# Relation layers with one group in three gathered, two filled from the node table, and the adjacency loop run by three groups

## The reference

```
src, dst = edge_index                         # 103125 edges, dst sorted
h = relu(layernorm(x))                        # 3125 x 128
for W, b, a, g, beta in three layers:         # node layers, 256 wide, and a fourth without the norm
    c = segment_sum((h @ W)[src] * norm, dst) + b
    h = elu(layernorm(c * sigmoid(a)) * g + beta)
x = x + fourth_layer(h)
y = relu(layernorm(x))
for l in range(3):                            # relation layers
    seg = dst * 16 + edge_type
    agg = segment_sum(y[src], seg) / max(count, 1)      # 3125 x 16 x 128
    y = einsum('nrd,rdo->no', agg, W[l]) + y @ root[l] + bias[l]
    y = relu(y) except in the last
out = x + y
```

## Time and profile before

| | us |
|---|---|
| median of 3 runs | 4118.48 (4111.23 to 4122.4) |
| the profiled execution | 4112.04 |
| its span | 4110.3 |
| TensorE busy in the span | 2902.5 (71%) |
| VectorE busy | 2243.8 (55%) |
| ScalarE busy | 1309.5 (32%) |
| GpSimd busy | 1214.9 (30%) |
| relation layers, start to end of the span | 1643 to 4110 |

### The profile page before, as it was taken

The page is one execution under the profiler, slowest core; times in us unless marked ns, Lnnn a source line. Parts: engine busy times, 40 slices in busy tenths (PEclk is TensorE's granted clock), DMA queues, the critical chain, the costliest instruction groups (busy, mean ns, idle before and its releaser), DMA issues.

```text
span 4110.3 us, 80589 instructions
## 1 busy us (share of the span) xinstructions
PE 2902.5 (71%) x25480; PEld 1920.3 (47%) x25481; DVE 2243.8 (55%) x7967; ACT 1309.5 (32%) x3058; POOL 1214.9 (30%) x1251
## 2 busy tenths in 40 slices
PE   3214776777799897677777777777777767777777
PEld 1112333333455554455555555555555545555555
DVE  6667888885634433354445444445444444544444
ACT  0315777775322210222222222222222222222221
POOL 1020000000000000354545543544454444445443
PEclk8557889888899999898999999999999999999999
DMA  0001000001101012533333334333333333333332
GB/s 21 0 23 52 36 36 36 36 36 50 52 20 46 20 51 58 156 112 99 101 115 105 101 91 123 104 109 108 101 102 111 103 105 102 113 101 100 114 100 74
DMA packets 164628, 320.93 MB, mean 78 GB/s; under 512 B 33105, under 2 KB 127676, under 8 KB 154924
## 3 DMA queue, kind: packets, MB, share of 16 engines
q1 hardware_dynamic: 123532, 231.88, 18.2%
q0 software_dynamic: 40992, 87.70, 7.9%
HBM read 274.51 MB, written 44.96 MB: 78 GB/s over the span
## 4 chain that ended last, share of the span: by engine, by line
PE 24%; issue 10%; DMA 10%; DVE 8%; POOL 6%; another core or an unknown queue 1%; DVEq 1%; ACT 0%; SPq 0%; POOLq 0%; ACTq 0%
DMA arena<-pair,arena 9%; PE psum L1922 8%; PE psum L1933 7%; PE psum L1942 6%; POOL arena L1846 6%; DVE arena L2090 3%; DVE arena L2086 3%; DVE arena L2123 1%; DVE arena L2096 1%; PE psum L1903 1%; PE psum L1911 1%; PE psum L1880 1%; DVEq L2123 0%; PE psum L1887 0%
## 5 line engine op out<-in xcount | busy, mean ns | idle before, releaser
L1846 POOL DMA_INDIRECT arena<-pair,arena x1212 | 1162.7, 959 | 1280.9 <-PE psum L1911 655.5
L2034 ACT ACTIVATE arena<-psum 128x512 f16<-128x512 f32 x909 | 477.3, 598 | 1663.4 <-PE psum L1911 1040.3
L1922 PE MATMUL psum<-arena 128*128 128x320 f16 x2424 | 445.1, 334 | 554.5 <-DMA arena<-pair,arena 318.0
L2096 DVE SCALAR_TENSOR_TENSOR arena<-psum,arena,work 128x320 f32<-128x320 f32 x606 | 329.3, 548 | 739.5 <-PE psum L1933 340.0
L1933 PE MATMUL psum<-arena 128*128 128x320 f16 x4242 | 680.7, 316 | 0.0
L1922 PEld LDWEIGHTS psum<-arena 128*128 128x128 f16 x2424 | 232.5, 106 | 733.1 <-issue 589.9
L1933 PEld LDWEIGHTS psum<-arena 128*128 128x128 f16 x4242 | 440.7, 104 | 201.9
L1090 PE MATMUL psum<-arena,h 128*128 128x512 f16 x1750 | 487.2, 384 | 23.5 <-ACT work L1144 15.5
L2090 DVE TENSOR_SCALAR arena<-arena 128x320 f16<-128x320 f16 x2121 | 484.9, 297 | 0.0
L1942 PE MATMUL psum<-arena 128*128 128x160 f32 (+1 forms) x2496 | 359.2, 303 | 50.7 <-issue 36.9
L1091 PE MATMUL psum<-arena,h 128*128 128x128 f16 x1750 | 386.7, 221 | 0.0
(11 more groups left out here) (260 smaller groups left out, 3303.8 us busy)
## 6 DMA issues: line engine op xcount, KB each, us to landing
work<-winv SPq DMA_DIRECT2D x75, 1280.0 KB, 6.2
arena<-pull SPq DMA_DIRECT2D x303, 224.0 KB
pull<-rows SPq DMA_DIRECT2D x101, 224.0 KB
arena<-pair,arena POOLq DMA_INDIRECT x1212
h<-work SPq DMA_DIRECT2D x12, 640.0 KB, 3.3
h<-h POOLq DMA_DIRECT2D x12, 640.0 KB, 7.4
pair<-arena SPq DMA_DIRECT2D x12, 256.0 KB
x_pad<-arena SPq DMA_DIRECT2D x1, 1600.0 KB, 7.3
```

The costliest lines, as they stand in the source:

```text
L1846: e.indirect_dma_start(out=t.msg[:, j, k].rearrange("p h f -> p (h f)"), out_offset=None, in_=d[f"pair_{l}"].rearrange("n h f -> n (h f)") ...
L1922: m = e.matmul(p.psum[:, 0, 0:KEYS], t.msg[:, j, tile, half, :], t.oh[:, j % 2, tile, :], start=(tile == 0 and half == 0), stop=(tile == G ...
L2034: e.activation(t.smsg[:, q, 2 * b:2 * b + 2].rearrange("p k h f -> p (k h f)"), p.psum[:, GATHER + b, :], ACT.Copy).then_inc(s_gv, 1)
L2096: e.scalar_tensor_tensor(t.agg[h][:, :, k % BATCH, :], p.psum[:, k % 2, 0:KEYS].rearrange("p (r w) -> p r w", r=REL), t.back[:, l:l + 1], ...
```

## The change

Three stages are rewritten, and two follow from that.

**Relation layers.** Groups come in threes: one gathered, two filled. 67 threes and one gathered group make a layer, so 68 groups are gathered (101 before) and 134 filled (101 before). The order on TensorE in a three is `sums_gathered`, a fill, `sums_filled`, a fill, `sums_filled`. A turn is 12 groups (4 threes, `TURN`), an apply takes 6 groups (`BATCH`); there are 16 turns and a rest of 10 groups. The first apply of a turn stands in the third three, behind its first fill. POOL gathers two threes ahead: two tiles after `sums_gathered` of three j-2, two after the second fill of three j-2. The sums go to the two banks in turn, and VectorE writes the one-hots in three parts between the means.

**Adjacency loop.** Three groups in an iteration, two of them with slots. ScalarE makes all one-hots of sources. 134 slot matrices are written instead of 101.

**Slots.** All arrays grow from 101 to 134 filled groups.

**Node layers.** ScalarE copies the first half of the products of group i+1 ahead of its work on group i, with a semaphore of its own (`s_z`), and the exponential, the ELU sum and the high half are done in two parts (2 and 3 blocks).

```diff
-PAIRS = EDGE_TILES // GT // 2
+TRIPLES = EDGE_TILES // GT // 3
+FILLED = 2 * TRIPLES
...
-BATCH = 8
-HALF = BATCH // 2
+BATCH = 6
 TURN = 2 * BATCH
-TP = TURN // 2
+TT = TURN // 3
+HALF = TT // 2
+FT = 2 * TT
...
# POOL, relation layers
-        def gathers(l, turn, ready, pairs):
-            held(e, s_pk, ready, passed)
-            for j in pairs:
-                filled = turn * TP + (l * PAIRS + j + 1)
-                summed = turn * TURN + (MM0 + l * NG + 2 * j)
+        def gathers(l, turn, h):
+            held(e, s_pk, turn * 6 + (l * PICKS + 3 * h + 1), passed)
+            for j in range(h * HALF, h * HALF + HALF):
+                summed = turn * TURN + (MM0 + l * NG + 3 * (j - 2) + 1)
+                filled = turn * FT + (GA0 + l * FILLED + 2 * (j - 2) + 3)
                 for k in range(GT):
                     if k == 0:
+                        held(e, s_mm, summed, passed)
+                    if k == 2:
                         held(e, s_ga, filled, passed)
-                    elif k == 2:
-                        held(e, s_mm, summed - 1, passed)
...
# TensorE, relation layers
-            def pairs_of(turn, pairs, ahead):
-                for j in range(pairs):
-                    if j < ahead:
-                        fill(turn, j + 1, PIECES * j)
+            def triples_of(turn, triples, fills):
+                for j in range(triples):
                     sums_gathered(turn, j)
-                    sums_filled(turn, j)
-                    if j % HALF == HALF - 1 or j == pairs - 1:
-                        apply(turn, j // HALF, 2 * (j % HALF + 1))
+                    fill(turn, 2 * j + 1, PIECES * 2 * j)
+                    if j == HALF:
+                        apply(turn, 0, BATCH)
+                    sums_filled(turn, j, 0)
+                    if 2 * j + 2 <= fills:
+                        fill(turn, 2 * j + 2, PIECES * (2 * j + 1))
+                    sums_filled(turn, j, 1)
...
             with e.Fori(0, TURNS) as i:
-                pairs_of(i, TP, TP)
+                triples_of(i, TT, FT)
+                apply(i, 1, BATCH)
...
# VectorE, relation layers
+        def triples_of(l, turn, triples, hots):
+            for j in range(triples):
+                more, gather_more = j + 1 < hots, j + 1 < hots or triples == RT
+                mean(l, turn, 3 * j)
+                if gather_more:
...
+                    hots_gathered((j + 1) % TT)
+                if j == HALF:
+                    adds(l, turn, 0, BATCH)
+                mean(l, turn, 3 * j + 1)
+                if more:
+                    hots_filled((j + 1) % TT, 0)
+                mean(l, turn, 3 * j + 2)
+                if more:
+                    hots_filled((j + 1) % TT, 1)
...
# VectorE, adjacency loop
+        def trio(i, more):
+            e.load(regs, t.gbase[0:1, bass.ds(i * 3, 3)])
+            keys(i * 3 + 2, 2)
+            adds(i * 3, 0)
+            slot_hots(i * 2)
+            keys(i * 3 + 3, 0)
+            adds(i * 3 + 1, 1)
+            slot_hots(i * 2 + 1)
+            ones(i * 2)
+            slot_keys(i * 2, 0)
+            if more:
+                keys(i * 3 + 4, 1)
+            adds(i * 3 + 2, 2)
+            ones(i * 2 + 1)
+            slot_keys(i * 2 + 1, 1)
...
# TensorE, adjacency loop
-        with e.Fori(0, ROUNDS // 2) as i:
-            for par in range(2):
-                r = i * 2 + par
-                turn(r + 1, 1 - par)
-                slot_keys(r, par)
-                place(r + 1, 1 - par)
+        with e.Fori(0, TRIPLES) as i:
+            turn(i * 3 + 1, 1)
+            place(i * 2, 0)
+            turn(i * 3 + 2, 2)
+            slot_keys(i * 2, 0)
+            place(i * 2 + 1, 1)
+            turn(i * 3 + 3, 0)
+            slot_keys(i * 2 + 1, 1)
...
# ScalarE, node layers
+            for k in range(KH):
+                sums(0, k)
             for i in range(GROUPS):
+                early = i + 1 < GROUPS and (KH == 1 or i + 2 < GROUPS)
+                if early:
+                    sums(i + 1, 0)
                 group(i, stays and i == GROUPS - 1)
+                if i + 1 < GROUPS:
+                    for k in range(1 if early else 0, KH):
+                        sums(i + 1, k)
```

More of the change, by code:

```diff
@@ L810, in _, with sources @@
+        trio(TRIPLES - 1, False)
+        e.load(regs[0:1], t.gbase[0:1, ROUNDS - 1:ROUNDS])
+        adds(ROUNDS - 1, 0)
     @block.scalar
     def _(e):
-        e.sem_inc(s_ct, 2 * G)
-        e.sem_inc(s_src, 2)
-        def sources(r, par):
+        e.sem_inc(s_ct, 3)
+        e.sem_inc(s_src, 3)
+        def sources(r, pos):
             held(e, s_st, r + 2, passed)
-            held(e, s_src, r + 2, passed)
-            for k in range(ASCAL):
-                e.activation(t.away[:, k, :], t.iota_h[:, 0:P], ACT.Abs, bias=t.stage[:, par, 0, k:k + 1],
+            held(e, s_src, r + 3, passed)
+            for k in range(GT):
+                e.activation(t.away[:, k, :], t.iota_h[:, 0:P], ACT.Abs, bias=t.stage[:, pos, 0, k:k + 1],
@@ L842, in _, with trio @@
+        def trio(i, more):
+            take(i * 3, 0)
+            sources(i * 3 + 2, 2)
+            take(i * 3 + 1, 1)
+            take_placed(i * 2, 0)
+            sources(i * 3 + 3, 0)
+            take(i * 3 + 2, 2)
+            take_placed(i * 2 + 1, 1)
+            if more:
+                sources(i * 3 + 4, 1)
         sources(0, 0)
         sources(1, 1)
-        with e.Fori(0, (ROUNDS - 3) // 2) as i:
-            for par in range(2):
-                r = i * 2 + par
-                take(r, par)
-                take_placed(r, par)
-                sources(r + 2, par)
@@ L873, in place, with turn @@
-        def place(r, par):
-            e.wait_ge(s_slot, r * GT + GT)
-            e.wait_ge(s_sk, r + 1)
-            for c0, c1, bank in ((0, 512, 4 + 2 * par), (512, SLOTS, 5 + 2 * par)):
+        def turn(r, pos):
+            e.wait_ge(s_src, r + 4)
+            e.wait_ge(s_key, r * GT + GT + 1)
+            e.wait_ge(s_ct, r + 1)
+            for k in range(GT):
+                m = e.matmul(p.psum[:, pos, 0:WIDE], t.oh_s[pos][:, k, :], t.oh_k[pos][:, k, :],
+                             start=(k == 0), stop=(k == GT - 1))
+            m.then_inc(s_mm, 1)
@@ L1744, in relations, with got @@
     block = Bodies()
[L1746 to L1748 removed]
+    def got(l, turn):
+        return 16 * GT * (l * (TURNS + 1) + turn + 1)
     def uses(slot):
[L1752 removed]
+        return len(range(slot, FILLED, G_AHEAD))
     @block.sync
@@ L2054, in _ @@
                 takes(i, HALF)
-            takes(TURNS - 1, RP - HALF)
-            for j in range(1, RP):
-                take(TURNS, j)
+            takes(TURNS - 1, RT - HALF)
+            for m in range(1, 2 * RT):
+                take(TURNS, m)
             if not last:
@@ L2143, in _ @@
             with e.Fori(0, TURNS) as i:
-                for h in range(2):
-                    means(l, i, h, HALF, TP)
-                    adds(l, i, h, BATCH)
-            for h, pairs in ((0, HALF), (1, RP - HALF)):
-                means(l, TURNS, h, pairs, RP - 1)
-                adds(l, TURNS, h, 2 * pairs)
+                triples_of(l, i, TT, TT + 1)
+                adds(l, i, 1, BATCH)
+            triples_of(l, TURNS, RT, RT)
+            mean(l, TURNS, 3 * RT)
+            adds(l, TURNS, 1, REST - BATCH)
             if last:
```

473 lines of the change are left out of this document (223 added, 250 removed).

## The result

The changed kernel takes 4379.07 us (median of 4 runs, 4374.40 to 4380.52), the kernel before 4118.40 beside it: 1.063 times as long (95% interval 1.0615 to 1.0651). It was forecast faster, at 3950. The span of its profiled execution is 4376.4 us.

A forecast was written before the change was run, and what follows sets the result against it. No engine is full: relation layers are a ring of fills, gathers and sums, while VectorE paces adjacency. From 4112.04: - 270 (relation) + 130 (adjacency) + 17 (slots) - 38 (node) = 3951, said as 3950; range 3850 to 4220.

The forecast's parts named there:

- Slots and node layers: Slots stage forecast 17 us longer (ends 5 and 22), node layers 38 us shorter (ends 10 and 60).
- the wait for the copies: Relation layers: the second fill waits for ScalarE's four copies of the first, losing 0.25 us, so a three takes 7.52.
- A turn: 3 x 7.52 + 7.27 + 4.0 + 0.65 + 4.0 = 38.5 us: Relation layers: four threes, two applies and one wait for the last mean make 12 groups at full clock.
- The "0.95" of the sum: Relation layers: granted clock taken from before, turning 38.5 us a turn into 40.5, 682 a layer, a gain of 270.
- 10.53 us of work: Adjacency loop: VectorE's queue for one trio of groups, counted from the old round's pieces; 67 trios are 706 us.
- 1.2 of stalls: Adjacency loop: VectorE stalls 0.9 us before `ones` and some 0.3 before the second `slot_keys` of a trio.
- Nothing of TensorE or ScalarE is that long: Adjacency loop: no other engine's work in a trio reaches VectorE's 10.53 us.
- the 11.7 of the prediction: Adjacency loop: us a trio with stalls, 786 us in all; 130 more than now was taken (ends 58 and 165).
- Rival 1: Relation layers: a gather being issued holds the fill's signal, a three takes 9.8 us, 4215 in all; chance 0.30.
- Rival 2: Relation layers: half the gain, an uncovered three takes 8.9 us, a gain of 150, about 4080 in all; chance 0.20.
- two signs of being wrong: The prediction is wrong if a relation-layer three is over 9.2 us, or the adjacency stage costs more than 200 us.
- the node layers' parts: Node layers: 17 us gained in the first and 20 in the others, given as 38 less.

The follow-up runs named there:

- b_node: The kernel before with only the changed kernel's node layers: 4077.75 us, 0.991 of before.
- a_pad1: The changed kernel with one unused word ahead of the two tables from which registers are loaded, three words behind them: 4038.25 us, 0.982 of before.
- a_again: The changed kernel run once more, word for word: 4306.02 us, 1.048 times before.
- a_warm: The changed kernel with eight unused matmuls on TensorE ahead of each adjacency trio's first place: 1.017 times before.
- a_quads: The changed kernel with the adjacency loop's windows table copied to four words a trio, so VectorE loads four registers from 16-byte addresses: 1.029 times before.
- a_order: The changed kernel with VectorE's queue in the adjacency loop put in another order: 1.028 times before.
- a_takes_only: The changed kernel with only ScalarE's adjacency queue reordered, copies of sums ahead of the one-hots of sources: 4315.85 us.
- a_takes: a_all with ScalarE's adjacency queue also reordered, copies of sums ahead of the one-hots of sources: 3859.87 us, 0.929 of before.
- a_four: The changed kernel with one word of padding and without POOL's wait between its second and third gather, so four are issued in a row: 4301.81 us, 1.045 times before.
- a_all: The changed kernel with one word of padding, the table of four words a trio and VectorE's new adjacency order together: 0.959 of before.

## Why the prediction was wrong

**Slots and node layers** were right: 16.5 us for 17, and 40.6 for 38, which b_node gives to that part alone.

**Relation layers: the pieces were right, an instruction was missing.** The fill, the sums, the apply and the wait for the copies are as counted, and with the table on 16 bytes a turn is 38.4 us for the 38.5 worked out at full clock. That is not luck: its four threes, the applies with them, are 7.52, 7.50, 10.96 and 12.46 us in a_pad1 (medians), for 7.52, 7.52, 11.27 and 12.17. The step that failed is "A turn: 3 x 7.52 + 7.27 + 4.0 + 0.65 + 4.0 = 38.5 us": it ends with the second apply and goes on with the next sum as if nothing lay between. The trace of before held a register load there, 1.62 us and nearly hidden, and no term asked what the change would do to it. The change lengthened arrays ahead of the table, and the load grew by 4.05 us in each of 48 turns. With what follows from half clock behind it that cost 266 us (2329.7 in a_again to 2063.7 in a_pad1). The "0.95" of the sum was mis-sized as well: with no gap the granted clock was 1.00, and the layers without the fault gained 407 us, not 270.

**Adjacency: VectorE's queue was right, its waits were not.** 10.53 us of work were forecast (9.9 measured) and 1.2 of stalls (1.24). The step "Nothing of TensorE or ScalarE is that long" failed. It compared busy times, where it holds (the window gives TensorE 9.3 and ScalarE 9.1 us a trio), but the trio is a ring: slot one-hots, the first place, slot one-hots again. TensorE stood idle before that place and ran it at half clock, 3.1 us where only 1.7 of VectorE's work lay beside it (1.84 of wait), and the loop's end with its slower load was 1.60. A trio is 15.03 us for the 11.7 of the prediction. a_warm and a_quads give half clock and load their size (1.4 and 0.64 us), a_order and a_takes_only show that a new order of one queue leaves the ring closed, and a_takes opens it.

**Rival 1** was right about the mechanism and wrong about this kernel. A gather under way can hold the signal, and four in a row cost 264 us (a_four). With the gathers in twos the first fill's signal was late in 82 of 201 threes in the first session and in 6 in the other, 75 us apart. It explains a part of the gap to the forecast in the first result, not the larger part.

**Rival 2** asked for a three of 8.9 us; it is 7.83 in the rows above, and 7.50 in a_again.

Of the prediction's two signs of being wrong, the one on the adjacency stage came true (357 us for its 200); the one on the three did not, and none looked at the loop's end. Two small slips change nothing: the node layers' parts add up to 37, not 38, and by rival 1's own sum a three of 9.2 us makes a turn of 43.6, not 43.9.

With both causes mended the changed design does gain: a_takes is 7.1% faster than before in its session, 3860 us (the spans of the two traces differ by 6.2%). The changed kernel with one word of padding and nothing else (a_pad1) is 1.8% faster.

## What to carry to other kernels

Count what stands at a loop's end as carefully as the work in it: register loads run on the engine's own queue, aren't counted as busy, and stay hidden only while the work in flight is longer than they are. When arrays in a hand-made layout change their size, look up where each table that registers are loaded from comes to stand. A busy time shorter than the period is no proof that an engine can be left out: write the iteration as a ring of who waits for whom, with TensorE's pieces at half clock where its idle time has brought that (the first place here, after 3.33 us), and know that a new order of one queue can show nothing until the queue that it shares the ring with is mended too. Where gathers are issued while another engine waits for a signal, two at a time cost less here than four in a row (a_pad1 and a_four).

## What the runs showed of the hardware

- By these times a load of registers from SBUF reads 16 bytes at once where the address allows it. 24 registers: 1.62 us from an address on 16 bytes, 5.67 from 4 or 8 bytes off. On VectorE four registers on 16 bytes cost 0.35 us in a_quads and a_all, one costs 0.32, and six 1.41 off the boundary and 0.81 on it (a_pad1). The queue's order matters as well: the four take 0.61 us in a_takes, three take 1.01 in the changed kernel and 0.75 in a_order; why is open. The Trainium skill (Runtime: NRT & Kernel Launch, Instruction fetch mechanics) gives some 200 ns a register for loads from HBM even in bulk; off the boundary these rows have 236 ns, on it 67.
- With a gather being issued, TensorE's signal can be raised one to three us late (in the row of a_four the copies start 1.3 us past the gather's end, 2510.02 to 2511.31), nearly always when it is the third or fourth in a row (276 of 278). None of 833 fills that ended without a gather under way had its copies late. The longest of these waits stand in the profile as "remote" or as a transfer long past.
- The same program took 4379 and 4306 us in two sessions, each within 0.2%, with 30 and with one wait put down to "remote" in their traces; the kernel before moved from 4111 to 4155 in the sessions.
